# Graph network kernel: a ring of lo one-hots, adjacency and convolution in one Block, an unsplit scatter and f32 queries

## The reference

```python
deg = segment_sum(1, dst) ; dinv = rsqrt(deg)          # with self loops
h = leaky(batchnorm(x @ W1 + b1)); h = h / norm(h)
for _ in range(5):
    m = h @ W
    agg = segment_sum(m[src] * dinv[src] * dinv[dst], dst) + bias
    h = leaky(batchnorm(agg))
x = layernorm(x + h / norm(h))
Q, K, V = x @ wq + bq, x @ wk + bk, x @ wv + bv         # 8 heads of 16
ef = edge_attr @ we + be                                # 200000 x 64 by 64 x 128
es = exp((Q[src] * (K[dst] + ef)).sum(-1) / 4)
out = segment_sum(es / denom[src] * V[dst], src) @ wo + bo
x = layernorm(x + out)
```

## Time and profile before

| | |
|---|---|
| median of 3 runs | 5244.65 us |
| profiled execution: its own time | 5247.15 us |
| profiled execution: span | 5245.6 us |
| mean granted TensorE clock | 0.942 of full |
| busy, share of the span | PE 73%, DVE 65%, POOL 65%, ACT 32% |

### The profile page before, as it was taken

How to read it: one execution, slowest core, us unless ns; L and a number is a source line. 1 busy time by engine, 2 the same in 40 slices (tenths; PEclk the granted TensorE clock), 3 DMA queues, 4 the chain that set the end, 5 groups by cost and what they waited for, 6 DMA issues and landing times. The chain is left out here.

```text
span 5245.6 us, 95577 instructions
## 1 busy us (share of the span) xinstructions
PE 3828.0 (73%) x24852; PEld 2425.0 (46%) x24853; DVE 3410.0 (65%) x10241; ACT 1665.9 (32%) x4208; POOL 3435.8 (65%) x3648
## 2 busy tenths in 40 slices
PE   5346666666639999999999857676666667676664
PEld 3112222222224454545454436666666666666664
DVE  8999999999921120202020168887887878878787
ACT  0056666666620010101010123333333333333332
POOL 2067777777777777777730017777777777777773
PEclk8889999999969999999999979999999999999998
DMA  9322332322379999898978634444444444444442
GB/s 365 119 85 92 102 128 90 139 90 95 134 185 327 321 310 336 295 337 290 337 270 291 197 105 131 131 131 131 132 132 131 131 130 131 132 131 132 131 131 77
DMA packets 363179, 929.25 MB, mean 177 GB/s; under 512 B 75929, under 2 KB 193549, under 8 KB 361192
## 3 DMA queue, kind: packets, MB, share of 16 engines
q1 hardware_dynamic: 203136, 552.41, 31.6%
q0 software_dynamic: 143520, 317.62, 21.4%
q10 hardware_dynamic: 16400, 57.93, 2.9%
HBM read 727.27 MB, written 200.43 MB: 177 GB/s over the span
## 5 line engine op out<-in xcount | busy, mean ns | idle before, releaser
L749 POOL DMA_INDIRECT records<-recs,poss x1562 | 1626.5, 1041 | 552.8 <-issue 544.0
L1380 POOL DMA_INDIRECT kv<-kv_table,rec x1616 | 1552.5, 961 | 497.4 <-issue 465.4
L909 PE MATMUL ps<-adj,mh 128*128 128x500 f16 (+1 forms) x6370 | 1315.4, 366 | 0.0
L1418 PE MATMUL ps<-msg,ohf 128*128 128x136 f32 x3232 | 504.1, 301 | 636.8 <-DVE msg L1478 635.5
L582 PE MATMUL ps<-h 128*128 128x490 f16 x2500 | 651.5, 385 | 399.4 <-ACT h L683 342.0
L909 PEld LDWEIGHTS ps<-adj,mh 128*128 128x128 f16 x6370 | 619.8, 97 | 686.4 <-issue 35.8
L1063 DVE SCALAR_TENSOR_TENSOR h<-ps,vecs,deg (+1 forms) x65 | 46.7, 718 | 1120.3 <-PE ps L909 1120.3
L537 DVE TENSOR_SCALAR h<-iota,rel 128x490 f16<-128x490 f16 x2500 | 774.0, 370 | 0.0
L1418 PEld LDWEIGHTS ps<-msg,ohf 128*128 128x128 f32 x3232 | 418.8, 196 | 712.8 <-DVE msg L1478 364.4
L582 PEld LDWEIGHTS ps<-h 128*128 128x128 f16 x2500 | 200.7, 99 | 850.3 <-ACT h L683 555.8
L1444 ACT ACTIVATE msg<-scores 128x32 f32<-128x32 f32 x404 | 92.6, 229 | 1288.8 <-DVE scores L1473 1288.8
(11 more groups left out here) (262 smaller groups left out, 4519.6 us busy)
## 6 DMA issues: line engine op xcount, KB each, us to landing
adj<-adj_full SPq DMA_DIRECT2D x420, 875.0 KB, 5.9
adj_full<-blk SPq DMA_DIRECT2D x12, 6125.0 KB
records<-deg ACTq DMA_DIRECT2D x1, 56576.0 KB, 198.1
rec<-records SPq DMA_DIRECT2D x404, 136.0 KB
recs<-in_edge_attr POOLq DMA_DIRECT2D x142, 352.0 KB, 5.6
kv<-kv_table,rec POOLq DMA_INDIRECT x1616
records<-recs,poss POOLq DMA_INDIRECT x1563
adj<-adj_tail SPq DMA_DIRECT2D x35, 437.5 KB, 3.7
```

Source lines behind the costliest of these rows:

```text
L749: G.indirect_dma_start(out=k.rec_d, out_offset=bass.IndirectOffsetOnAxis(ap=k.poss[:, q, j:j + 1], axis=0), in_=k.recs[:, q, j, :], in_off ...
L909: last = mm(bank, mh[:, part, hi, :], adj[:, c, x * width:(x + 1) * width], start=False, stop=True, skip_group_check=True)
L1380: G.indirect_dma_start(out=kv[:, q, j, :], out_offset=None, in_=k.kv_d, in_offset=bass.IndirectOffsetOnAxis(ap=rec[:, q, j, RD:RD + 1].bit ...
L1418: last = mm(PS[:, 6 + q % S, j // 2 * MW:(j // 2 + 1) * MW], ohf[:, q, j, :], msg[:, q, j, :], start=(j % 2 == 0), stop=(j % 2 == 1))
```

## The change

- **Ring.** The lo one-hots of all tiles are made once, in order, into a ring of 50 slots (`ohl`), with the first three slots copied behind the last so that four in a row can always be read. DVE makes them by tensor-scalar with the f32 lo of the tile (`spread`), 12 tiles ahead; ACT makes three pairs per group (`distances`, `onehots`), between its copies. PE reads the ring at an offset from the table. The ring and the tables lie in the memory of `deg` and `h`.
- **Codes.** The code one-hot compares a slice of a table of 1960 codes (four phases of 490) with `code` directly; the four subtractions are gone. `prepare` makes the codes to suit, with a cast, two tensor-scalars and a scalar-tensor-tensor more.
- **Table.** Two running scans (least and most) take the place of the masked products; five counts on DVE and five sign passes on ACT give first and last tiles. A few more small steps find whether the ring's distances hold.
- **One Block.** The adjacency programs run at the head of the convolution's Block; SP raises `graph_stored` when the stores have landed, and the engines wait for that. The degrees go to DRAM block by block, and the trip at the start of the convolution begins with the load.
- **Scatter.** Unsplit, in steps of 22 tiles with two slots; the next step's load and copies are issued after five scatters of the current one, once the scatters of the slot's last step have landed.
- **Queries.** Q is kept in f32 (`qn`), the splits are gone, the turned one-hot is written as f32, and one f32 product per 128 edges takes the place of three bf16 ones.

```diff
-TW = 16
+TW = 24
+RING = 50
+AHEAD_LO = 12
+TWO = 25
+PAIRS = 3
...
-RR = 4
-SG = 11
+RR = 2
+SG = 22
...
-                adjacency(k)
-            if upto >= 3:
-                convolve(k)
+                graph_programs = adjacency(k)
+            convolve(k, graph_programs)
...
                 v.wait_ge(mm_loaded, 32)
...
-                for j in range(WPP):
-                    V.scalar_tensor_tensor(m[0:WP, 0:T], tmn[0:WP, 0:T], w4[0:WP, 0, j:j + 1], up[0:WP, 0:T], ALU.is_lt, ALU.mult)
-                    L(V.scalar_tensor_tensor(n[0:WP, 0:T], tmx[0:WP, 0:T], thr[0:WP, j:j + 1], down[0:WP, 0:T], ALU.is_ge, ALU.mult))
-                    V.tensor_reduce(w4[0:WP, 1, j:j + 1], m[0:WP, 0:T], AX.X, ALU.max)
-                    L(V.tensor_reduce(w4[0:WP, 2, j:j + 1], n[0:WP, 0:T], AX.X, ALU.max))
...
+                V.tensor_tensor_scan(least[0:WP, ::-1], tmn[0:WP, ::-1], tmn[0:WP, ::-1], float(N), ALU.min, ALU.min).then_inc(sem("least_ready"), 1)
+                L(V.tensor_tensor_scan(most[0:WP, :], tmx[0:WP, :], tmx[0:WP, :], 0.0, ALU.max, ALU.max))
...
+                for j in range(WPP):
+                    V.tensor_scalar(eq[0:WP, j % 2, 0:T], most[0:WP, 0:T], thr[0:WP, j:j + 1], None, ALU.is_lt, ALU.add,
+                                    accum_out=w4[0:WP, 1, j:j + 1]).then_inc(starts, 1)
...
-                        for x in range(WPP):
-                            last = V.tensor_scalar(rel[:, par, x, :], k.code[:, bass.ds(first[x], FAST)], wbase[:, bass.ds(w + x, 1)], None, ALU.subtract)
...
-                            lo_onehots(ohl[:, q, 0:JV[x], :], first[x], JV[x])
...
-                            for j in range(FAST):
-                                last = V.tensor_scalar(ohc[:, q, j, :], iota[:, :], rel[:, par, x, j:j + 1], None, ALU.is_equal)
...
+            def spread(t, i=None):
+                slot = t % RING
+                of_tile = k.lo[:, t:t + 1] if i is None else k.lo[:, bass.ds(i * (2 * TWO) + t, 1)]
+                for q in (slot, slot + RING) if slot < FAST - 1 else (slot,):
+                    V.tensor_scalar(ohl[:, q * P:(q + 1) * P], codes[:, 0:P], of_tile, None, ALU.is_equal)
...
+                    for x in range(WPP):
+                        q, f = (w0 + x) % SL, (w0 + x) % PH
+                        v.wait_ge(done, w + x + 1)
+                        for j in range(FAST):
+                            last = V.tensor_scalar(ohc[:, q, j, :], codes[:, f * WC:(f + 1) * WC], k.code[:, bass.ds(first[x] + j, 1)], None, ALU.is_equal)
+                        last.then_inc(ready, 1)
...
+                pe.wait_ge(ready_lo, gr * PAIRS + PAIRS)
...
+                            last = nc.tensor.matmul(PS[:, q, 0:WC], ohl[:, bass.ds(at[x] + j * P, P)], ohc[:, q, j, :],
+                                                    start=(j == 0), stop=(j == FAST - 1))
...
+                    if more:
+                        t = of_act((q if loop is not None else b) * GB + g + 1)[x]
+                        if x == 0:
+                            act.wait_ge(done, (b * GB + g) * WPP + SL)
+                        distances(t, loop, x)
...
+                    put_window(b * BW + y, q, y, (q * BW + y) % SL)
+                    if more:
+                        onehots(t, x, nth)
+                    if y == 4 and (type(b) is not int or b > 1):
+                        take(b - 2, q, BD)
...
         for j in range(SG):
+            if j == FETCH and more:
+                if type(i) is not int or i > 0 or nq == 0:
+                    g.wait_ge(sent[nq], 16 * SG * (i + (nq == 0)))
+                fetch(step + 1, nq)
...
-                        for part in range(3):
-                            mm(PS[:, 2 + q % S, j * P:(j + 1) * P], oht[:, q % S, j, :],
-                               k.q3[:, bass.ds(b[j // 2], 1), part, :].rearrange("p a c -> p (a c)"), start=(part == 0), stop=(part == 2))
+                        mm(PS[:, 2 + q % S, j * P:(j + 1) * P], oht[:, q % S, j, :],
+                           k.qn[:, bass.ds(b[j // 2], 1), :].rearrange("p a c -> p (a c)"), start=True, stop=True)
```

More of the change, by code:

```diff
@@ L33 @@
 NW = N // WD
-WCODE = 512
+PH = 4
 BW = 50
@@ L719, with tiles_of, of_act, table @@
-SPLIT = 17
-def scatter_records(k, g, lo, hi):
+        summed, deg_free, deg_moved = sem("degrees_summed"), sem("degrees_taken"), [sem("degrees_out0"), sem("degrees_out1")]
+        def tiles_of(g):
+            return AHEAD_LO + g * TWO // 2
+        def of_act(g):
+            return range(tiles_of(g + 1) - 2 * PAIRS, tiles_of(g + 1), 2)
+        def table(engine, gr, at, most):
+            _, values = nc.values_load_multi_w_load_instructions(
+                k.wt[0:1, bass.ds(gr * TW + at, WPP + 1)], engines=(engine,), min_val=0, max_val=most,
+                skip_runtime_bounds_check_because="the program has made the table within these bounds")
+            return values
@@ L731, in scatter_records, with fetch @@
     rounds, left = NS // RR, NS % RR
-    def load(step, q):
+    def fetch(step, q):
         g.dma_start(k.recs[:, q, :, 0:F], attr[:, bass.ds(step * SG, SG), :]).then_inc(loaded[q], 16)
+        G.tensor_copy(k.recs[:, q, :, RD:RL + 1].bitcast(I32), k.dl[:, bass.ds(step * SG, SG), :])
+        G.tensor_copy(k.poss[:, q, :], k.pos[:, bass.ds(step * SG, SG)]).then_inc(copied, 1)
     def step_of(i, q, more=True):
         step, nq = i * RR + q, (q + 1) % RR
-        if more:
-            if type(i) is not int or i > 0 or nq == 0:
-                g.wait_ge(sent[nq], 16 * SG * (i + (nq == 0)))
-            load(step + 1, nq)
-        c0 = step * SG
-        G.tensor_copy(k.recs[:, q, :, RD:RL + 1].bitcast(I32), k.dl[:, bass.ds(c0, SG), :])
-        G.tensor_copy(k.poss[:, q, :], k.pos[:, bass.ds(c0, SG)]).then_inc(copied, 1)
         g.wait_ge(loaded[q], 16 * (i + 1))
@@ L776, in convolve @@
-def convolve(k):
+    for q in range(left):
+        step_of(rounds, q, q < left - 1)
+    q = RR - 1
+    g.wait_ge(sent[q], 16 * SG * rounds)
+    g.dma_start(k.recs[0:TE, q, 0, 0:F], k.io["edge_attr_64"][TF * P:E, :]).then_inc(loaded[q], 16)
+    G.tensor_copy(k.recs[:, q, 0, RD:RL + 1].bitcast(I32), k.dl[:, TF, :])
+    G.tensor_copy(k.poss[:, q, 0:1], k.pos[:, TF:TF + 1]).then_inc(copied, 1)
+    g.wait_ge(copied, NS + 1)
+    g.wait_ge(loaded[q], 16 * (rounds + 1))
+    G.indirect_dma_start(out=k.rec_d, out_offset=bass.IndirectOffsetOnAxis(ap=k.poss[0:TE, q, 0:1], axis=0),
+                         in_=k.recs[0:TE, q, 0, :], in_offset=None).then_inc(sent[q], 16)
@@ L782, in convolve @@
+    for q in range(RR):
+        g.wait_ge(sent[q], 16 * SG * (rounds + (q < left)) + (16 if q == RR - 1 else 0))
+def convolve(k, graph):
     nc, sem, PS, io = k.nc, k.sem, k.ps, k.io
@@ L1247, in bias @@
                     V.tensor_tensor(kvs[:, n % 2, t % 4:t % 4 + m, :], PS[:, 4 + t % 4:4 + t % 4 + m, D:3 * D], spread(bkv, m), ALU.add).then_inc(biased, 1)
[L1249 to L1259 removed]
+                for x in range(len(pairs)):
+                    bias(x)
 LEAD = 8
```

593 lines of the change are left out of this document (291 added, 302 removed).

## The result

The changed kernel takes 5113.5 us (median of 4 runs, 5106.2 to 5115.0) against 5246.2 for the kernel before beside it: a ratio of 0.9744 (95% interval 0.9727 to 0.9760). The forecast of 4974 and the range of 4900 to 5090 missed it: the sign was right, the gain half of what was foretold.

The account below looks back on a forecast made before the run. DVE was taken to bound the adjacency build, PE the convolution, POOL the attention. Build -245, prepare -10.7, code table +2.1, One Block -13 and project -4 sum to -270.6; 5247.15-270.6-2.5 = 4974 us, range 4900 to 5090.

Parts of the forecast that it names:

- Build: Adjacency build: 795 us of DVE work, 87 of contention and 32 of waits make 914 against 1159, -245 us.
- Waits: DVE's waits in the build, mostly at block edges: 43 us before, 32 after, bounds 10 and 60.
- DVE's own work: Adjacency build: 920 lo one-hots at 152 us plus 2500 code one-hots at 643 us, 795 us.
- the contention: Adjacency build: what POOL costs DVE, 0.15 us for each of 586 scatters, 87 us, bounds 60 and 130.
- with about a microsecond to spare: Adjacency build: PE (6.2 us upper bound) and ACT (5.0 to 6.0) fit under 7.3 us a group.
- Prepare and the code table: Ahead of the build: prepare's passes replaced by scans and counts, -10.7 us; POOL's longer table of codes, +2.1 us.
- One Block: Between build and convolution: POOL's Block-end wait and the small degree store leave the chain, -13 us (bounds -8 and -16).
- Project: Queries in f32: DVE loses 50 splits and ACT 50 copies in project, -4 us (0 to -7).
- Attention: Eight f32 products for twelve bf16 add 0.24 us a group on PE, hidden by POOL's gathers: 0.
- POOL's last scatter: Scatter in steps of 22, 1.56 us per scatter during the build, ends near 2530, convolution near 2727: 200 us of cover.
- Rival 1: Adjacency build: ACT with PE takes over at 8.2 us a group, build 1025, kernel 5085; chance 0.16.
- rivals 2 to 5: Freer build 4915 (0.16); code one-hots lose fast mode 5274 (0.04); scatter slots wait 5116 (0.06); f32 queries uncovered 5054 (0.07).

Follow-up runs that it names:

- e1: VectorE's never-entered branch for long windows taken out of its build loop, against the changed kernel with two data-given values made constant; 5031.9 us.
- e3: Never-entered branches for long windows taken out on both VectorE and TensorE, against the changed kernel with two data-given values made constant; 5053.6 us.
- e8: e3 with the last 10 of its 71 scatter steps left out (220 of 1562 scatters); 5007.9 us.
- e6b: e1 with the scatter held back so that none runs in the build; 5537 us (one run), build 886.3.
- e5b: Kernel before, with data-given values made constant, and 20 no-operations put in each never-entered branch; 5269.1 us, ratio 1.0045.
- e2: TensorE's never-entered branch for long windows taken out of its build loop, against the changed kernel with two data-given values made constant; 5092.1 us.
- e10b: Changed kernel with constants, long-window fallback moved to a second build loop on VectorE and TensorE, four pairs on ScalarE; 5026.1 us, ratio 0.9567.

## Why the prediction was wrong, point by point

The trace's spans differ by 132.4 us; the forecast had 270.6.

- **Build, -245 forecast, -99 measured: the wrong term.** The step that failed is "Waits: 43 us before ... so I take 32, bounds 10 and 60". DVE stood idle for 163.5 us: 102 for its own instructions, 59 for PE. DVE's own work of 795 was measured as 797.4, the contention forecast as 87 is 99. The 43 us of waits before were a remainder, put down to block edges; the trace has 51.5, of them 18.6 with no releaser, all ahead of L528, which the prediction didn't look at. e1 shows that 95 us of such gaps go with some 120 instructions that this data never executes; the prediction counted executed instructions and never the length of the loop. It had also written that PE and ACT fit "with about a microsecond to spare", without the load of six registers that PE's group begins with.
- **Prepare and the code table, -8.6 forecast, -12.4 measured.** The first lo one-hot starts at 271.78 in place of 284.17.
- **One Block, -13 forecast, -16.7 measured.** From the last code one-hot to the convolution's first product 95.1 us, before 111.9.
- **Convolution 0: measured -0.3.** Project -4: measured -2.5. Attention 0: measured -1.3. Eight f32 products took 0.19 us a group more than twelve bf16 ones (416.9 against 346.2 us in 375 groups; foretold 0.24), hidden by POOL as argued.
- **POOL's last scatter "near 2530", with 200 us of cover: wrong, and by luck without a price.** It ended at 2707, with 155 us left to the products' end, so nothing was lost. But had the build come out at 914, the cover would have been gone: in e3, at 934, the scatter ends 99 us after the products. A scatter was taken at 1.56 us in the build, with the mean of the old build as its base; it is 1060.0/556 = 1.91 in the kernel after and 934.5/368 = 2.5 in e3, since some are held up for 5.7 us. So there were two errors, and the second would have cost its share had the first not been made (e3: 5054). With 220 scatters left out and a build of 946, e8 takes 5008; 32 us less, for a build of 914, would be 4976 as an estimate, near the 4974 of the forecast: the terms outside the build were right within 4 us each.
- **Rivals.** Rival 1 (PE or ACT takes over) has part of the truth, at 59 us of PE; rivals 2 to 5 did not occur. None was a loop that is fetched anew.

The Trainium skill, in "SBUF — State Buffer", section "Who interferes with whom", has the shared port as a lock that blocks either side wholly; the prediction applied it to DVE alone. The scatters of 5.7 us in place of 0.97 show POOL's side. In the Trainium skill's rule the lock lasts for one instruction; here the scatters last as long as a row of 20.

Open: why 76 instructions of padding bring the kernel before 40 us of gaps and 0.45%, while 120 less relieve the changed one of 95 us of gaps and of 84 us in all; what decides which scatters are held up; why the runs at 6273 us and more lose time beside the scatter; and what a PE that reads its table one group ahead would give, since it wasn't tried.

## What to carry to other kernels

Where an edit adds code inside a loop, count the instructions of one pass, with the branches never taken, before counting their time: here a loop of 365 instructions in place of 245 cost VectorE 95 us of gaps. Look at what the sequencer does at the head of each group (register loads, branches) and at what transfer runs beside it. Look at the median and the longest of a group beside its mean. And when one engine gets denser, price the other side of the contention, and ask whether the work that it delays is still covered.

## What the runs showed of the hardware

- A loop of 245 instructions on DVE had 7 to 9 us of gaps without releaser in its whole build (e1, e3, e6b, e8), one of 290 18.6 us. One of 365 had 102 us, with gaps of up to 8 us at the edges of its passes, one of 366 (e5b) 58 us. On PE 1369 instructions branched back in 0.2 us, 1561 and more in 3.5 to 4.6 (medians of five).
- A load of six registers takes 1.48 us on PE, 0.82 on DVE, and up to 6.4 and 4.0 (e2, e10b) while 6 MB are stored.
- GpSimd's scatter takes 0.97 us. Beside 20 tensor-scalar one-hots of VectorE in a row some take 5 to 6 us: the mean is 1.11 us in the kernel before, where none does, 1.37 after and 2.02 in e3.
